# Six expert numbers packed into a word: 13 register loads ahead of the first expert loop in place of one in every tile

## The chip, the cores and the metric

The kernel runs on one core of one Trainium2 chip. The metric is the device time of one execution in microseconds, the median over several runs; lower is better. The core has five engines with an instruction stream each: TensorE (PE, with PEld for its weight loads), VectorE (DVE), ScalarE (ACT), GpSimd (POOL) and SyncE (SP, which only issues transfers here). They meet through semaphores alone: an instruction can raise one when it is complete, and another engine can wait for its value.

## What is computed

A small multimodal network over 16 sequences of 126 tokens (49 image patches and 77 words), 2016 tokens of 128 values: patch embedding, attention, a mixture of 16 experts, a two-layer LSTM-like recurrence, and a second layer of 8 experts. The change is in the first mixture of experts, which the reference writes like this (cut to what matters; `xf` holds the 2016 normalized tokens, and `h` has 512 values):

```
tw = _routing_weights(xf, Wr, br, Wgate, bgate)   # 2 of 4 groups, 2 of 4 experts in each
for e in range(16):
    h = silu(xf @ W1[e]) * (xf @ W3[e])
    out = out + tw[:, e:e + 1] * (h @ W2[e])
```

Every token therefore has four pairs with an expert, 8064 pairs in all.

## The kernel before, in words

**Routing.** The kernel sorts the 8064 pairs by expert into NT = 78 tiles of 128 rows, in such a way that a tile belongs to one expert. DVE works out in `route` how many tiles each expert gets; line 1128 leaves, for each tile on a partition of its own, the tile's expert times 2*W0 = 3072, which is where the expert's weights begin in the array `w0s`. PE turns that column into a row in PSUM (line 910, `EXPERT`). DVE and POOL then build one-hot matrices for 64 combinations of pick and token tile (lines 1141 to 1149 and 855 to 858), PE multiplies them into a table in PSUM (line 917), and from it DVE works out which rows of `x_scratch` each tile gathers (`src_row`, lines 1162 and 1163) and to which rows of `y_scratch` its result goes (`dst_row`, line 1171). Right behind the one-hot loop, at line 1152, DVE casts the row of expert offsets to integers (`expert_at`).

**The expert loop.** It is written out, not a hardware loop: 78 tiles, with every engine's instructions in an order fixed by hand. For tile i, PE waits for the transposed rows, computes the gate product (lines 937 to 939 into bank 0 or 1, raising `gate_ps`) and the up product (the same lines into bank 2 or 3, raising `up_ps`), each of three matmuls of 512 columns; then it transposes the hidden values of tile i - 1 (line 947) and multiplies those of tile i - 2 by the down weights (lines 957 and 958, raising `y_ps`). It also transposes the gathered rows of tile i + 2 (line 926, `xT_ps`), before the gate product. The matmuls read the weights at an address in a register. So PE's sequencer, the part of the engine that takes the instructions in order and hands them on, loads one offset from `expert_at` in each tile, after the up product (`expert_of`, line 930, called at line 983), and computes addresses from it with small register operations.

ACT copies the transposed rows (line 1016), applies silu (line 1033) and copies the high half of the transposed hidden values (line 1022). DVE multiplies gate and up (line 1220), forms the low half (line 1202), and adds the two halves of the down result into one of four buffers (`keep`, line 1209). PE's down product of tile i waits for `keep` of tile i - 1 (line 953), since both use one PSUM bank. POOL alternates between two indirect transfers: it fetches the rows of a tile five ahead (`fetch`, line 863) and gives the result of a finished tile (`give`, line 868). Two kinds of side work ride in the loop: in 4 early tiles ACT and DVE split weights of late experts (lines 427 and 437), and in 7 later tiles, nine apart, they split the weights of the recurrence (lines 1045 and 1231).

Behind the loop SP reads the results back, ACT and DVE mix them (lines 1051 and 1244), and the recurrence follows.

Of the kernel before, what the change touches and what calls it, by code (L numbers as in the profile page):

```python
# [18 lines left out]
I32 = mybir.dt.int32  # L19
# [53 lines left out]
YR = 4  # L73
DOWN_LAG = 2
# [16 lines left out]
def build(nc, taps_in, patches_in, txt_in, cols_in, const_in, dense_in, qkvw_in, outw_in, heads_in, w0_in,  # L91
# [5 lines left out]
    with ExitStack() as ctx:  # L97
# [123 lines left out]
        expert_at = view(NT, 1).bitcast(I32)  # L221
# [663 lines left out]
        def ffn_pe(pe):  # L885
# [25 lines left out]

            for c in range(COMBOS):
                pe.wait_ge(sg("off_hot"), c + 1)
# [15 lines left out]
            def expert_of(i):  # L929
                return nc.values_load(expert_at[0:1, i:i + 1], engines=(mybir.EngineType.PE,), min_val=0,  # L930
                                      max_val=(E0 - 1) * 2 * W0,
                                      skip_runtime_bounds_check_because="expert_f is the minimum with the last expert")
# [28 lines left out]
            pe.wait_ge(sg("route_dve"), AFTER["expert_at"])  # L961
# [36 lines left out]
        def ffn_act(act):  # L998
# [3 lines left out]
            for j in range(NBLK):  # L1002
# [6 lines left out]
                           ).then_inc(sg("route_exp"), 1)  # L1009
            act.activation(warm[:, :], warm[:, :], ACT.Silu)  # L1010
# [43 lines left out]
        def route(dve):  # L1054
# [73 lines left out]
            dve.tensor_scalar(expert_f[:, 1:2], expert_f[:, 0:1], float(E0 - 1), float(2 * W0), ALU.min, ALU.mult  # L1128
# [12 lines left out]
            for c in range(COMBOS):  # L1141
                if c >= COMBOS // 2:
                    t = c % TILES
                    dve.tensor_scalar(tile_hot[:, c, :], count16[0:SEQ, 0:NT], place[:, 1, c:c + 1],
                                      number(N_TOK + t, 1, SEQ), ALU.is_equal, ALU.mult)
                dve.tensor_scalar(off_hot[:, c, :], count16[0:SEQ, :], place[:, 2, c:c + 1], None, ALU.is_equal
                                  ).then_inc(sg("off_hot"), 1)
                if c % 4 == 0 and c < 4 * NBLK:
                    rows_low(c // 4)

            dve.wait_ge(sg("route_pe"), AFTER["expert_ps"])
            dve.tensor_copy(expert_at, EXPERT[0:1, 0:NT]).then_inc(sg("route_dve"), 1)
# [746 lines left out]
```

## Time and profile before

| what | value |
| --- | --- |
| median of 3 runs | 1110.24 us (1110.03 to 1111.13) |
| the profiled execution's own time | 1110.15 us |
| its span, first to last instruction | 1108.2 us |
| PE busy | 896.5 us, 81% of the span |
| DVE busy | 784.1 us, 71% |
| ACT busy | 556.8 us, 50% |
| POOL busy | 331.9 us, 30% |
| mean granted TensorE clock | 0.923 |

The span is what the trace shows, and 1.95 us of the execution lie around it. All times in the rows further down are microseconds from the start of the span unless marked ns. "PEldq" is the sequencer of PE; its instructions (register loads, register operations, waits) are not counted as busy. A row of a group gives the busy time, the mean of one instruction in ns, and the idle time of the engine just before, with what ended it. "<-remote" means that the idle time ended with a semaphore's update that no instruction ending near that moment explains. The clock is a share of full speed: 1.00 is 2.4 GHz and 0.50 is 1.2 GHz, and a figure between them is a stretch with some of each.

### The profile page before, as it was taken

To read this page: it belongs to the slowest core of one execution; us is meant where nothing else is said; L and a number is where in the kernel's file an instruction comes from. 1 tells how busy PE (TensorE), PEld (TensorE's weight loads), DVE (VectorE), ACT (ScalarE), POOL (GpSimd) and SP (SyncE) were. 2 spreads that over 40 slices of the span, in tenths; PEclk is the share of its full clock that TensorE was granted. 3 is DMA by queue.
4 is the path that set the end of the run, shared out by engine and by line. 5 is a ranking of instruction groups with operands and counts; after the bars stand their busy time and mean duration, and the time that the engine had idled before them with its cause. 6 is when DMAs were issued, how large, how long until landed. Compare 5 with 4: busy or idle time off the path is not lost.

```text
span 1108.2 us, 43614 instructions
## 1 busy us (share of the span) xinstructions
PE 896.5 (81%) x17230; PEld 721.4 (65%) x17230; DVE 784.1 (71%) x2835; ACT 556.8 (50%) x1629; POOL 331.9 (30%) x481
## 2 busy tenths in 40 slices
PE   3667768267787788773599999999999999989997
PEld 1346545135555555551489999999999988847786
DVE  3458984986655555556678888887788888755877
ACT  0446667125455444532354455555544455545886
POOL 0326656555565565540001111111111111020321
PEclk9769997569999998995699999999999999998999
DMA  8700005201222221216000000000000000002232
GB/s 237 271 1 2 1 30 171 62 25 38 65 66 63 65 65 44 59 34 160 19 4 0 0 0 0 0 0 0 0 0 0 0 0 0 1 2 87 94 140 75
DMA packets 26707, 52.07 MB, mean 47 GB/s; under 512 B 4528, under 2 KB 17816, under 8 KB 26648
## 3 DMA queue, kind: packets, MB, share of 16 engines
q1 hardware_dynamic: 21656, 41.04, 11.3%
q0 software_dynamic: 4992, 10.23, 3.5%
q8 instruction: 38, 0.62, 0.2%
q14 instruction: 21, 0.17, 0.0%
HBM read 44.02 MB, written 7.24 MB: 46 GB/s over the span
## 4 chain that ended last, share of the span: by engine, by line
PE 38%; DVE 10%; issue 7%; ACT 0%; DMA 0%; POOL 0%; DVEq 0%; ACTq 0%
PE quad L1330 19%; PE bank L1330 8%; DVE post L1480 3%; DVE post L1518 2%; PE quad L318 1%; PE bank L318 1%; PE quad L320 1%; PE quad L319 1%; DVE post L1524 1%; PE bank L319 1%; PE bank L320 1%; DVE post L1519 1%; PE quad L1340 1%; PE quad L1628 1%; PE bank L1360 0%
## 5 line engine op out<-in xcount | busy, mean ns | idle before, releaser
L1330 PE MATMUL quad<-post,area 128*128 128x32 f16 (+1 forms) x7520 | 230.2, 182 | 24.7 <-DVE post L1524 18.1
L1330 PEld LDWEIGHTS quad<-post,area 128*128 128x128 f16 x7520 | 213.1, 96 | 41.6 <-DVE post L1524 41.3
L1330 PE MATMUL bank<-post,area 128*128 128x32 f16 (+1 forms) x6260 | 193.2, 180 | 6.7 <-DVE post L1524 4.4
L1330 PEld LDWEIGHTS bank<-post,area 128*128 128x128 f16 x6260 | 176.9, 96 | 12.3 <-DVE post L1524 5.0
L1417 ACT ACTIVATE post<-post 128x96 f32<-128x96 f32 x252 | 71.3, 283 | 171.1 <-DVE post L1480 171.1
L1313 POOL COPY post<-post 128x32 f32 (+1 forms) x126 | 30.8, 245 | 381.8 <-DVE post L1524 381.8
L868 POOL DMA_INDIRECT y_scratch<-area x78 | 76.9, 985 | 88.7 <-DVE area L1209 78.6
L1508 DVE SCALAR_TENSOR_TENSOR post<-post 128x32 f32<-128x32 f32 x252 | 48.4, 192 | 75.6 <-ACT post L1427 75.6
L957 PE MATMUL quad<-w0s,area 128*128 x312 | 61.6, 277 | 49.2 <-DVE area L1209 49.2
L1480 DVE TENSOR_REDUCE post<-bank 128x96 f32<-128x192 f32 x252 | 80.7, 320 | 6.4 <-PE bank L1330 4.8
L1220 DVE SCALAR_TENSOR_TENSOR area<-bank,area 128x512 f32<-128x512 f32 x78 | 53.9, 691 | 43.8 <-ACT area L1033 21.3
L863 POOL DMA_INDIRECT area<-x_scratch,area x78 | 76.1, 975 | 28.1 <-issue 17.4
L1480 DVE TENSOR_REDUCE post<-quad 128x96 f32<-128x192 f32 x252 | 80.7, 320 | 5.3 <-PE quad L1330 3.8
L1016 ACT ACTIVATE area<-quad 128x256 f16<-128x256 f16 x78 | 29.9, 383 | 102.6 <-PE quad L926 59.4
L1422 ACT ACTIVATE post<-post 128x32 f32<-128x32 f32 x252 | 57.7, 229 | 29.3 <-DVE post L1480 0.2
L1202 DVE TENSOR_TENSOR area<-quad,area 128x512 f16<-128x512 f32 x78 | 53.5, 686 | 26.8 <-issue 14.4
L1427 ACT ACTIVATE post<-post 128x32 f32<-128x32 f32 x252 | 57.8, 229 | 28.1 <-DVE post L1494 0.2
L957 PEld LDWEIGHTS quad<-w0s,area 128*128 128x128 f16 x312 | 30.8, 99 | 62.1 <-issue 58.5
L1022 ACT ACTIVATE area<-quad 128x512 f16<-128x512 f32 x78 | 46.8, 600 | 41.4 <-PE quad L947 34.8
L1736 DVE TENSOR_TENSOR hidL<-area,hidH 128x504 fp32r<-128x504 f32 x64 | 49.8, 778 | 21.4 <-ACT hidH L1693 19.8
L937 PE MATMUL bank<-w0s,area 128*128 x156 | 60.7, 389 | 0.0
L938 PE MATMUL bank<-w0s,area 128*128 x156 | 60.5, 388 | 0.0
(255 smaller groups left out, 1940.4 us busy)
## 6 DMA issues: line engine op xcount, KB each, us to landing
w0s<-in_w SPq DMA_DIRECT2D x12, 768.0 KB, 12.3
area<-mask_scratch SPq DMA_DIRECT2D x7, 1008.0 KB, 4.6
area<-in_rec SPq DMA_DIRECT2D x7, 640.0 KB
post<-y_scratch SPq DMA_DIRECT2D x16, 252.0 KB
area<-in_w SPq DMA_DIRECT2D x4, 768.0 KB
post<-in_f SPq DMA_DIRECT2D x8, 256.0 KB, 4.4
area<-in_patches SPq DMA_DIRECT2D x1, 1488.4 KB
area<-in_taps SPq DMA_DIRECT2D x1, 1350.0 KB
```

The source lines that it names most:

```text
L863: pool.indirect_dma_start(xg[:, i % XG, :], None, x_dram, bass.IndirectOffsetOnAxis(src_row[:, i:i + 1].bitcast(mybir.dt.uint32), 0)).then ...
L868: pool.indirect_dma_start(y_dram, bass.IndirectOffsetOnAxis(dst_row[:, i:i + 1].bitcast(mybir.dt.uint32), 0), y_sb[:, i % YR, :], None).th ...
L937: pe.matmul(out, xh, wh, start=True, stop=False, skip_group_check=True)
L938: pe.matmul(out, xl, wh, start=False, stop=False, skip_group_check=True)
L957: pe.matmul(y_bank, hh, both, start=c == 0, stop=False, skip_group_check=True)
L1202: dve.tensor_tensor(hidT[:, i % 2, 1, :], hidT_bank[i % 2], hidT[:, i % 2, 0, :], ALU.subtract).then_inc(sg("hid_low"), 1)
L1220: dve.scalar_tensor_tensor(out=hid[:, i % 2, :], in0=bank[2 + i % 2], scalar=HID_SCALE / (H_SCALE * W_SCALE), in1=silu[:, i % 2, :], op0=A ...
L1330: mm = pe.matmul(at[0][:, at[1] + out.start:at[1] + out.stop], rec_w[:, w, s, m * P:(m + 1) * P], operand, start=False, stop=False, skip_g ...
L1417: act.activation(gates[:, l, 0:3 * SW], pre[:, l, 0:3 * SW], ACT.Tanh, scale=UNSCALE).then_inc(sg(f"gates{l}"), 1)
L1422: act.activation(gates[:, l, OUT:OUT + SW], pre[:, l, 3 * SW:4 * SW], ACT.Sigmoid, scale=UNSCALE)
L1427: act.activation(tanh_c[:, l], gates[:, l, CELL:CELL + SW], ACT.Tanh, scale=0.5).then_inc(sg(f"tanh_c{l}"), 1)
L1480: dve.tensor_reduce(pre[:, l, lo * BATCH:(lo + count) * BATCH].rearrange("p (m b) -> p m b", b=BATCH), src[:, 0:count * 64].rearrange("p ( ...
```

## The change

The offsets are no longer premultiplied: line 1128 leaves the expert's number. ACT, after PE's transpose of the expert row, multiplies every sixth entry by 16 to the power of its place (six copies of 13 elements from PSUM). DVE, after the one-hots of combination 16, adds six neighbours to one number and casts the 13 sums to integers; the cast at line 1152 goes. PE, after the table's 32nd matmul, waits for that cast and loads the 13 words into 13 registers. In the loop `expert_of(i)` is now a shift, a mask with 15 and a product with 3072 on a register, in place of a load.

```
--- before.py
+++ after.py
@@ -71,6 +71,7 @@
 XW2 = 2 * D
 XG, LOOK = 7, 5
 YR = 4
+WORD = 6
 DOWN_LAG = 2
 WHOLE = float(3 << 22)
 
@@ -218,7 +219,9 @@
         src_row = view(NT).bitcast(I32)
         dst_row = view(NT).bitcast(I32)
         expert_f = view(2, SEQ)
-        expert_at = view(NT, 1).bitcast(I32)
+        expert_row = view(NT, 1)
+        expert_sum = view(NT // WORD, 1)
+        expert_at = view(NT // WORD, 1).bitcast(I32)
         PAIR_AT = at[0]
 
 
@@ -909,7 +912,14 @@
             pe.wait_ge(sg("route_dve"), AFTER["expert_f"])
             pe.transpose(EXPERT[0:1, 0:SEQ], expert_f[:, 1:2], ident[0:SEQ, 0:SEQ]).then_inc(sg("route_pe"), 1)
 
+            words = ()
             for c in range(COMBOS):
+                if c == COMBOS // 2:
+                    pe.wait_ge(sg("route_dve"), AFTER["expert_at"])
+                    words = [nc.values_load(expert_at[0:1, w:w + 1], engines=(mybir.EngineType.PE,), min_val=0,
+                                            max_val=E0 ** WORD - 1,
+                                            skip_runtime_bounds_check_because="six experts of four bits each")
+                             for w in range(NT // WORD)]
                 pe.wait_ge(sg("off_hot"), c + 1)
                 if c < COMBOS // 2:
                     pe.wait_ge(sg("tile_hot"), c + 1)
@@ -927,9 +937,8 @@
                 mm.then_inc(sg("xT_ps"), 1)
 
             def expert_of(i):
-                return nc.values_load(expert_at[0:1, i:i + 1], engines=(mybir.EngineType.PE,), min_val=0,
-                                      max_val=(E0 - 1) * 2 * W0,
-                                      skip_runtime_bounds_check_because="expert_f is the minimum with the last expert")
+                return pe.snap((words[i // WORD] >> 4 * (i % WORD) & E0 - 1) * (2 * W0), min_val=0,
+                               max_val=(E0 - 1) * 2 * W0)
 
             def up(i, out, wh, wl, name):
 
@@ -958,7 +967,6 @@
                     mm = pe.matmul(y_bank[:, 0], hl, both[:, 0], start=False, stop=c == C0 - 1, skip_group_check=True)
                 mm.then_inc(sg("y_ps"), 1)
 
-            pe.wait_ge(sg("route_dve"), AFTER["expert_at"])
             pe.wait_ge(sg("w_low"), len(LOW_POOL))
             pe.wait_ge(sg("w_low_dve"), len(LOW_DVE) - len(LATE))
             at_of = {0: expert_of(0)}
@@ -1007,6 +1015,12 @@
             act.wait_ge(sg("route_dve"), AFTER["logit_shift"])
             act.activation(prob.rearrange("p n k -> p (n k)"), prob.rearrange("p n k -> p (n k)"), ACT.Exp
                            ).then_inc(sg("route_exp"), 1)
+            act.wait_ge(sg("route_pe"), AFTER["expert_ps"])
+            for k in range(WORD):
+                ins = act.activation(expert_row.rearrange("p (w k) -> p k w", k=WORD)[:, k],
+                                     EXPERT[0:1, 0:NT].rearrange("p (w k) -> p k w", k=WORD)[:, k], ACT.Copy,
+                                     scale=float(E0 ** k))
+            ins.then_inc(sg("route_exp"), 1)
             act.activation(warm[:, :], warm[:, :], ACT.Silu)
 
             def turned(i):
@@ -1125,7 +1139,7 @@
                                           op0=ALU.mult, op1=ALU.add))
             link(dve, dve.tensor_scalar(tiles(3), tiles(4), number(N_TOK, 1, SEQ), None, ALU.is_lt))
             link(dve, dve.tensor_reduce(expert_f[:, 0:1], tiles(3), AX, ALU.add))
-            dve.tensor_scalar(expert_f[:, 1:2], expert_f[:, 0:1], float(E0 - 1), float(2 * W0), ALU.min, ALU.mult
+            dve.tensor_scalar(expert_f[:, 1:2], expert_f[:, 0:1], float(E0 - 1), None, ALU.min
                               ).then_inc(sg("route_dve"), 1)
             for k in range(PICKS):
                 ins = dve.scalar_tensor_tensor(out=spread_pos[:, k * EW:(k + 1) * EW], in0=code,
@@ -1145,11 +1159,13 @@
                                       number(N_TOK + t, 1, SEQ), ALU.is_equal, ALU.mult)
                 dve.tensor_scalar(off_hot[:, c, :], count16[0:SEQ, :], place[:, 2, c:c + 1], None, ALU.is_equal
                                   ).then_inc(sg("off_hot"), 1)
+                if c == COMBOS // 4:
+                    dve.wait_ge(sg("route_exp"), 2)
+                    link(dve, dve.tensor_reduce(expert_sum, expert_row.rearrange("p (w k) -> p w k", k=WORD), AX, ALU.add))
+                    dve.tensor_copy(expert_at, expert_sum).then_inc(sg("route_dve"), 1)
                 if c % 4 == 0 and c < 4 * NBLK:
                     rows_low(c // 4)
 
-            dve.wait_ge(sg("route_pe"), AFTER["expert_ps"])
-            dve.tensor_copy(expert_at, EXPERT[0:1, 0:NT]).then_inc(sg("route_dve"), 1)
             dve.wait_ge(sg("route_exp"), 1)
             link(dve, dve.tensor_reduce(top_p[:, 0, :], prob, AX, ALU.add))
             link(dve, dve.reciprocal(top_p[:, 1, :], top_p[:, 0, :]))
```

## Rows read from the trace of the kernel before

**Rows 1.** The page: its first line.

```profile
span 1108.2 us, 43614 instructions
```

**Rows 2.** Busy time by stretch: bounds, length, PE, PEld, DVE, ACT, POOL; clock, DMA.

```profile
417.72:425.23 7.51, 7.51 (x63) 5.34 (x61) 4.54 (x9) 3.93 (x8) 4.99 (x6) 1.00 0.17 47
289.21:292.82 3.61, 2.67 (x23) 1.73 (x21) 3.61 (x7) 1.58 (x3) 1.95 (x3) 1.00 0.19 46
258.34:262.15 3.81, 2.68 (x24) 1.73 (x21) 3.81 (x6) 1.58 (x3) 1.97 (x3) 1.00 0.12 34
247.58:251.88 4.30, 2.71 (x24) 1.73 (x21) 4.30 (x6) 1.88 (x4) 1.99 (x3) 1.00 0.11 31
425.23:431.82 6.59, 3.58 (x24) 2.14 (x22) 3.00 (x5) 2.17 (x5) 3.22 (x5) 0.82 0.14 30
431.82:436.51 4.69, 4.69 (x22) 2.86 (x21) 1.52 (x3) 2.02 (x5) 2.78 (x3) 0.53 0.20 54
305.83:308.33 2.50, 2.50 (x23) 1.77 (x21) 1.81 (x4) 1.38 (x3) 1.89 (x3) 1.00 0.16 38
301.83:305.83 4.00, 2.67 (x23) 1.73 (x21) 1.62 (x3) 1.58 (x4) 2.01 (x3) 1.00 0.13 35
237.00:488.51 251.51, 203.44 (x1518) 135.15 (x1517) 147.93 (x253) 127.91 (x247) 144.54 (x148) 0.98 0.20 56
```

**Rows 3.** Who waited for whom, 237 to 496: us in total, times, longest.

```profile
PE quad L957 <- DVE area L1209: 49.2, 40, 2.6
...
DVE area L1209 <- remote: 33.3, 26, 1.6
```

**Rows 4.** Timeline from 301: start, duration, instruction, idle before it.

```profile
301.14 0.99 POOL L868 DMA_INDIRECT y_scratch<-area  x1 [0.30 <-issue]
...
301.66 0.22 PE L958 MATMUL quad<-w0s,area 128*128 x1
...
304.38 0.42 DVE L1209 TENSOR_REDUCE area<-quad 128x128 f32<-128x256 f32 x1 [1.61 <-remote]
304.42 0.38 ACT L1016 ACTIVATE area<-quad 128x256 f16<-128x256 f16 x1 [2.38 <-remote]
...
305.05 0.28 PE L957 MATMUL quad<-w0s,area 128*128 x1 [1.33 <-DVE area L1209]
```

**Rows 5.** PE's register load in three narrow stretches: min/median/max ns, first and last start.

```profile
L930 PEldq TENSOR_LOAD <-area x1: 298/298/298, 301.8 to 301.8; - x1
...
L930 PEldq TENSOR_LOAD <-area x1: 298/298/298, 306.2 to 306.2; - x1
...
L930 PEldq TENSOR_LOAD <-area x1: 297/297/297, 308.3 to 308.3; - x1
```

**Rows 6.** Timeline before and at the load at 306.2: POOL and ACT.

```profile
305.08 0.98 POOL L868 DMA_INDIRECT y_scratch<-area  x1 [1.69 <-DVE area L1209]
...
306.03 0.38 ACT L1016 ACTIVATE area<-quad 128x256 f16<-128x256 f16 x1 [0.25 <-PE quad L926]
```

**Rows 7.** PE's sequencer: all register loads; the register operations of one down product.

```profile
L930 PEldq TENSOR_LOAD <-area x78: 296/302/487, 227.9 to 486.1; - x78
...
L957 PEldq FUSED_REGOPS  x4: 46/46/46, 307.1 to 307.5; - x4
```

**Rows 8.** Timeline of the routing stage, 202 to 230.

```profile
202.58 0.37 PE L910 MATMUL bank<-const,area 126*1 126x126 f32 x1 [2.64 <-DVE area L1128]
...
210.49 3.39 DVE L1146 TENSOR_SCALAR area<-const,area 126x128 f16<-126x128 f16 x19
...
226.81 2.30 PE L917 MATMUL quad<-area 126*128 126x78 f16 x33 [0.40 <-DVE area L1146]
226.92 0.22 DVE L1152 CAST area<-bank 1x78 int32<-1x78 f32 x1
...
229.71 0.48 DVE L1162 TENSOR_REDUCE area<-quad 128x78 f32<-128x312 f32 x1
```

More of the change, by code:

```diff
@@ L73 @@
 YR = 4
+WORD = 6
 DOWN_LAG = 2
@@ L220, in build @@
         expert_f = view(2, SEQ)
-        expert_at = view(NT, 1).bitcast(I32)
+        expert_row = view(NT, 1)
+        expert_sum = view(NT // WORD, 1)
+        expert_at = view(NT // WORD, 1).bitcast(I32)
         PAIR_AT = at[0]
@@ L910, in ffn_pe @@
             pe.transpose(EXPERT[0:1, 0:SEQ], expert_f[:, 1:2], ident[0:SEQ, 0:SEQ]).then_inc(sg("route_pe"), 1)
+            words = ()
             for c in range(COMBOS):
+                if c == COMBOS // 2:
+                    pe.wait_ge(sg("route_dve"), AFTER["expert_at"])
+                    words = [nc.values_load(expert_at[0:1, w:w + 1], engines=(mybir.EngineType.PE,), min_val=0,
+                                            max_val=E0 ** WORD - 1,
+                                            skip_runtime_bounds_check_because="six experts of four bits each")
+                             for w in range(NT // WORD)]
                 pe.wait_ge(sg("off_hot"), c + 1)
@@ L929, in expert_of @@
             def expert_of(i):
-                return nc.values_load(expert_at[0:1, i:i + 1], engines=(mybir.EngineType.PE,), min_val=0,
-                                      max_val=(E0 - 1) * 2 * W0,
-                                      skip_runtime_bounds_check_because="expert_f is the minimum with the last expert")
+                return pe.snap((words[i // WORD] >> 4 * (i % WORD) & E0 - 1) * (2 * W0), min_val=0,
+                               max_val=(E0 - 1) * 2 * W0)
             def up(i, out, wh, wl, name):
@@ L1009, in ffn_act @@
                            ).then_inc(sg("route_exp"), 1)
+            act.wait_ge(sg("route_pe"), AFTER["expert_ps"])
+            for k in range(WORD):
+                ins = act.activation(expert_row.rearrange("p (w k) -> p k w", k=WORD)[:, k],
+                                     EXPERT[0:1, 0:NT].rearrange("p (w k) -> p k w", k=WORD)[:, k], ACT.Copy,
+                                     scale=float(E0 ** k))
+            ins.then_inc(sg("route_exp"), 1)
             act.activation(warm[:, :], warm[:, :], ACT.Silu)
@@ L1127, in route @@
             link(dve, dve.tensor_reduce(expert_f[:, 0:1], tiles(3), AX, ALU.add))
-            dve.tensor_scalar(expert_f[:, 1:2], expert_f[:, 0:1], float(E0 - 1), float(2 * W0), ALU.min, ALU.mult
+            dve.tensor_scalar(expert_f[:, 1:2], expert_f[:, 0:1], float(E0 - 1), None, ALU.min
                               ).then_inc(sg("route_dve"), 1)
```

7 lines of the change are left out of this document (4 added, 3 removed).

## The prediction

> **What bounds the kernel now.** I read four views: busy time by stretch for the pace of the expert loop, the list of waits for what breaks it, the timeline of one slow tile for the mechanism, and the sequencer's records for the register load. Durations are of the profiled execution, 1110.15 us with a span of 1108.2 [rows 1], 0.09 under the median.
>
> From the first gate matmul of tile 0 to that of tile 77, 77 tiles pass in 251.5 us, 3.27 each [rows 2]. A quick tile takes 2.50 us and PE is busy through all of it; so are three in a row with all of POOL's transfers going (7.51) [rows 2]. So 2.50 is PE's floor, 77 of them are 192.5, and 59.0 us lie above it. Taking the tiles one by one by the start of their first gate matmul, that excess divides as follows. 26 tiles take about 4.00 instead of 2.50, as the one at 301.83 does: 39.0. Seven carry a split of the recurrence's weights and take about 3.61, DVE busy throughout: 7.8. Four carry a split of late experts' weights, three of about 3.81 and one of 4.30: 5.7. Two in a row take 6.59 and 4.69, the clock going to 1.2 GHz for the second: 6.3 [rows 2]. The sum is 58.8.
>
> **The 26 tiles.** PE idles there before the down product and waits for DVE's `keep` [rows 3]. But `keep` needed only the previous down product, whose last matmul ran at 301.66 for 0.22 us; `keep` started at 304.38, and ACT's copy of the transposed rows, due at 302.0, at 304.42. Both waits end "remote" [rows 4]; DVE has 26 such before `keep`, 33.3 us in all [rows 3]. PE had done the work, then, and its semaphore updates arrived some 2.4 us late, several at once. In the rest of the kernel no wait is listed as remote.
>
> What sets these tiles apart is where the register load falls. At 301.8 it falls inside POOL's issue of a result, 301.14 to 302.13 [rows 4, 5]. At 306.2 it comes just after such an issue (305.08 to 306.06) has ended, and that tile runs at 2.50 [rows 2, 5, 6]. I laid all 78 loads beside POOL's instructions: in each of the 26 slow tiles the load overlaps a result issue, and in none of the tiles of 2.50, but for one at 422.7 just ahead of the two long ones. And the phase returns by itself: after a slow tile the load comes 0.37 after the tile's start (306.2 against 305.83), one quick tile later at its start (308.3 against 308.33) [rows 2, 5], which is inside the issue again. That is why slow and quick tiles mostly alternate. I take it that a load that meets a result issue holds back PE's updates.
>
> **The change, part by part.**
>
> *The loads in the loop go.* With the cause, the 26 holds go: 39.0. The two long tiles at 425 have late updates from PE too, the first from a load that begins just before an issue; I count them in, 6.3, less surely. The splits stay, 13.5. Gain 45.3. Next in line behind PE's 2.50 is POOL: two transfers of 0.98 with 0.30 before each [rows 4, 6] make 2.56 to 2.60 a tile. It looks ahead five tiles, and the eleven splits give it 13.5 us in which to catch up 77 x 0.08 = 6, so I charge nothing; without that cover 6 us come back.
>
> *Three register operations per tile are added.* Four stand within 0.4 us [rows 7], 0.13 apart, so three cost 0.39 of the sequencer's time, against 0.30 for a load and 0.06 to the next instruction. That is even, and the sequencer gains 0.37 on PE in a quick tile, as shown above, which covers it: nothing. If the operations weren't fused or were repeated for the down product, six would be 0.78, 0.42 more than the load, which uses that cover up and costs 0.05 a tile, 4 us in all.
>
> *Thirteen loads move ahead of the table's second half.* Its last 33 matmuls run together from 226.81 for 2.30 us, since POOL's and DVE's one-hots are done by then [rows 8]. PE's sequencer takes things in order, so the loads come after matmul 32 and push the other 32. Each takes 0.302 at the median [rows 7], 0.36 with the step behind it: 13 x 0.36 = 4.7. The table is then ready at 233.8 instead of 229.1. DVE began to read it at 229.71, 0.6 after it was ready [rows 8]; that slack stays, so 4.1 us reach DVE, POOL's first fetch and tile 0. Bounds: if loads overlap, no faster than register operations, 13 x 0.13 - 0.6 = 1.1; if each costs what the dearest did (0.487) and a step, 13 x 0.55 - 0.6 = 6.6. I take the median, since all but one lie near it. POOL issues no transfer there, so nothing should be held. The Trainium skill ("DMA: Bandwidth & Descriptors", latency and other measured facts) gives a load a floor of about 600 ns; the trace has half of that, and the trace decides. By that figure the estimate for the step would be 13 x 0.66 - 0.6 = 8 us and the forecast 4 us later.
>
> *ACT's six copies* start behind PE's transpose, done at 202.95 [rows 8]. At the 0.38 of a far larger copy [rows 4] they take 2.3 and end by 205.3. ACT has nothing urgent until the rows arrive. DVE asks for them after combination 16, past 210.49 [rows 8], so it doesn't wait; nothing is queued behind that wait in vain. DVE's sum and cast cost about 0.22 each, as the old cast did [rows 8], with links 0.6, less the 0.22 that goes: 0.4 later at the table. Its last one-hots then come 0.4 late too, at about 227.2, while PE is busy with the loads to 231.5: nothing. If the loads cost next to nothing, that 0.4 shows.
>
> *Sum:* -45.3 + 4.1 = -41.2; 1110.15 - 41.2 = 1069. Behind the loop nothing changes but the start.
>
> **Rivals.**
>
> *The holds come from POOL's issue alone.* A result issue of POOL would hold PE's updates whether a load is there or not, and the load's place only follows from the hold. Then the loop stays at 251.5, and the 4.1 us ahead of it are a loss: 1114. It decides if one quick tile in which an issue covers the down product's end is held without a load. Against it: in the quick tile of 305.83, PE's transpose ends just inside the issue of 305.08 to 306.06, and ACT goes on at 306.03 without delay [rows 6]. For it: both movers sit in one fixed order, so the phase isn't free in this trace. Beside it: the Trainium skill ("TensorE: Matmul & The Clock Gate", the per-tile semaphore tail) says that increments on completion go one after another, at 26.3 ns each, with no word of a load. Rows 4 show 2.4 us, and by that rule no load could be blamed, so that the time would be this rival's. 10%.
>
> *Half of it goes.* Holds become rarer or shorter but something late takes their place: fetches landing late, DVE's 1.8 busy of 2.50 meeting POOL's pace. A tile of 2.8 on average, 216 + 13.5 for the loop: 22 less, 18 net: 1092. For it: only short runs of quick tiles are seen. Against: in them PE never waits. 13%.
>
> *The sequencer becomes the bound.* If the mask and product were made anew at each use, eight uses x 0.39 = 3.1 us per tile minus the 0.36 and the cover of 0.37 give 2.4 more: 1069 + 185. The text of the change takes one register value per tile, which speaks against. 2%. That the words are reloaded in the loop after all, for want of registers, would leave about 1112. 2%.
>
> **How the numbers follow.** The forecast has 73%. Its own range is 1060 to 1080: below, the loads nearly free (-3) and the splits absorbed in part (-6); above, POOL's pace (+6), dear loads (+2.5) or six operations (+4), not all together. The stated range reaches to the second rival, 1060 to 1093, and leaves out the first and the dear ones. A measurement here tells about 0.2%, 2.2 us. Faster 87%, slower 11%, within it 2%.
>
> **What would show it.** Right: 13 loads at about 227 to 231, none later; the stretch of the loop at about 206 us; no wait ended remote; PE's idle before the down product near 11 us instead of 49.2 [rows 3]; DVE's L1162 near 233.9. Wrong: remote waits still there; quick tiles over 2.50 with PE waiting on sequencer ("issue"); a first gate matmul much later than 241.1.

## The result and the profile after

The changed kernel takes 1116.78 us (median of 6 runs, 1115.6 to 1121.57) where the kernel before takes 1110.55 beside it (6 runs, 1110.03 to 1112.88): a ratio of 1.0058, 95% interval 1.0038 to 1.0079 (a ratio, here and in the table below, isn't exactly that of the two medians). It is slower by some 6 us, where 41 us of gain were forecast. The profiled execution takes 1115.6 us.

The page of the changed kernel: its first line, and one of the costliest groups (busy time, mean ns of one | idle time before, and what ended most of it). L966 is the down product that was L957, L1225 `keep`; further down, L1030 is ACT's copy of the transposed rows, L866 and L871 are the fetch and the result that were L863 and L868.

```profile
span 1113.5 us, 43699 instructions
...
L966 PE MATMUL quad<-w0s,area 128*128 x312 | 61.1, 276 | 41.2 <-DVE area L1225 41.2
```

Busy time by stretch in the changed kernel, with the columns of [rows 2]: the loop from the first gate matmul of tile 0 to that of tile 77, then a quick tile, a slow one, one with a split of the recurrence's weights, and the two long ones.

```profile
246.09:494.78 248.69, 207.69 (x1519) 134.16 (x1517) 147.86 (x252) 127.56 (x247) 144.35 (x148) 0.98 0.21 56
251.37:253.87 2.50, 2.50 (x24) 1.78 (x21) 1.25 (x3) 1.65 (x4) 0.53 (x1) 1.00 0.16 51
303.92:307.85 3.93, 2.84 (x23) 1.68 (x21) 1.85 (x4) 1.99 (x5) 2.06 (x3) 1.00 0.13 34
297.77:301.41 3.64, 2.85 (x22) 1.71 (x21) 3.64 (x8) 1.58 (x3) 1.98 (x3) 1.00 0.24 50
432.52:439.53 7.01, 3.58 (x23) 2.12 (x21) 2.91 (x5) 1.85 (x4) 3.08 (x4) 0.89 0.14 28
439.53:442.94 3.41, 3.41 (x22) 2.03 (x21) 1.12 (x2) 1.55 (x4) 2.79 (x3) 0.73 0.21 61
```

The loop of 251.51 us [rows 2] is now 248.69: not 206. Who waited for whom in it, changed kernel:

```profile
ACT area L1030 <- remote: 41.3, 26, 2.3
PE quad L966 <- DVE area L1225: 41.2, 40, 3.3
DVE area L1225 <- remote: 33.0, 26, 1.6
```

The 26 remote waits of [rows 3] are still 26. One of them in the timeline of the changed kernel (start, duration, instruction, idle before it):

```profile
303.05 0.99 POOL L871 DMA_INDIRECT y_scratch<-area  x1 [0.30 <-issue]
...
303.75 0.22 PE L967 MATMUL quad<-w0s,area 128*128 x1
...
304.34 0.97 POOL L866 DMA_INDIRECT area<-x_scratch,area  x1 [0.30 <-issue]
...
306.17 0.42 DVE L1225 TENSOR_REDUCE area<-quad 128x128 f32<-128x256 f32 x1 [0.86 <-remote]
306.21 0.38 ACT L1030 ACTIVATE area<-quad 128x256 f16<-128x256 f16 x1 [1.63 <-remote]
...
306.84 0.28 PE L966 MATMUL quad<-w0s,area 128*128 x1 [1.02 <-DVE area L1225]
306.87 0.98 POOL L871 DMA_INDIRECT y_scratch<-area  x1 [1.56 <-DVE area L1225]
```

It is the picture of [rows 4] with no register load anywhere near. The down product's last matmul is over at 303.97; DVE hears of it at 306.17, 2.2 us later and 0.86 after the end of POOL's fetch issue (304.34 and 0.97). In [rows 4] it was 2.5 us. I call such a tile held. The loop is 2.8 us shorter because held tiles and the two long ones came out a little shorter in this execution. That isn't the change's doing. Over three profiles of each kernel the loop took 251.51, 247.57 and 247.24 us before (before_again and before_3, below) and 248.69, 249.42 and 248.73 after (after_again and after_3): the loads went from it, and it became no shorter.

Where the change put its loads, changed kernel: the sequencer's loads (min/median/max ns, first and last start), then PE and DVE.

```profile
L919 PEldq TENSOR_LOAD <-area x13: 295/302/479, 231.4 to 235.9; - x13
```

```profile
231.35 0.23 PE L927 MATMUL quad<-area 126*128 126x78 f16 x1 [0.39 <-DVE area L1160]
...
236.25 2.24 PE L927 MATMUL quad<-area 126*128 126x78 f16 x32 [4.67 <-issue]
...
238.59 0.48 DVE L1178 TENSOR_REDUCE area<-quad 128x78 f32<-128x312 f32 x1 [4.53 <-PE quad L927]
```

This part is as forecast: thirteen loads in 4.9 us, the table's second half behind them, and DVE idle for 4.53 us before it reads the table. Against [rows 8] that read comes 8.88 us later. Only 4.35 of these are the loads' and 0.4 the words' on DVE: the expert row's transpose, ahead of all that, already stands 4.14 later (206.72 against 202.58 [rows 8]):

```profile
206.72 0.37 PE L913 MATMUL bank<-const,area 126*1 126x126 f32 x1 [2.64 <-DVE area L1142]
```

That part is not the change's: in before_again and before_3, which are the kernel before, the same transpose starts at 206.59 and 206.67. By 190 us 3.5 of it are there, before anything that the change touches. The granted clock differs in that stage: 0.86 of full speed on average from 60 to 190 us before, 0.84 after.

```profile
60.00:190.00 130.00, 95.08 (x905) 70.10 (x906) 96.33 (x119) 87.29 (x168) 73.25 (x53) 0.86 0.13 44
```

```profile
60.00:190.00 130.00, 94.59 (x888) 69.51 (x889) 96.37 (x119) 84.06 (x166) 68.93 (x52) 0.84 0.12 42
```

(The first is the kernel before, the second the changed one.) That the clock is the cause is argued from these means, not shown. In any case this pair of profiles doesn't give the change's price; a cleaner one follows.

### The profile page after: what moved, and what is told of

Same layout as the page of the kernel before. It is cut to its first block, busy times and chain, and to the rows that moved or that the text cites. A ratio compares the mean times of both kernels' runs of the same rounds, so it can differ in the third digit from the quotient of the medians.

```text
span 1113.5 us, 43699 instructions
## 1 busy us (share of the span) xinstructions
PE 906.3 (81%) x17230; PEld 724.5 (65%) x17230; DVE 784.9 (70%) x2836; ACT 557.3 (50%) x1635; POOL 332.6 (30%) x481
## 4 chain that ended last, share of the span: by engine, by line
PE 37%; DVE 10%; issue 7%; ACT 1%; DMA 0%; POOL 0%; DVEq 0%; ACTq 0%
PE quad L1346 19%; PE bank L1346 8%; DVE post L1496 3%; DVE post L1534 2%; PE quad L321 1%; PE bank L321 1%; PE quad L323 1%; PE quad L322 1%; DVE post L1540 1%; PE bank L322 1%; DVE post L1535 1%; PE bank L323 1%; PE quad L1356 1%; PE quad L1644 1%; ACT post L1443 0%
## 5 line engine op out<-in xcount | busy, mean ns | idle before, releaser
L871 POOL DMA_INDIRECT y_scratch<-area x78 | 76.9, 985 | 86.1 <-DVE area L1225 76.0
L966 PE MATMUL quad<-w0s,area 128*128 x312 | 61.1, 276 | 41.2 <-DVE area L1225 41.2
L866 POOL DMA_INDIRECT area<-x_scratch,area x78 | 76.1, 975 | 32.5 <-issue 17.4
L1030 ACT ACTIVATE area<-quad 128x256 f16<-128x256 f16 x78 | 29.9, 383 | 102.4 <-PE quad L936 58.6
L966 PEld LDWEIGHTS quad<-w0s,area 128*128 128x128 f16 x312 | 30.6, 98 | 54.2 <-issue 50.6
L947 PE MATMUL bank<-w0s,area 128*128 x156 | 60.2, 386 | 0.0
```

The costliest lines, as they stand in the source:

```text
L866: pool.indirect_dma_start(xg[:, i % XG, :], None, x_dram, bass.IndirectOffsetOnAxis(src_row[:, i:i + 1].bitcast(mybir.dt.uint32), 0)).then ...
L871: pool.indirect_dma_start(y_dram, bass.IndirectOffsetOnAxis(dst_row[:, i:i + 1].bitcast(mybir.dt.uint32), 0), y_sb[:, i % YR, :], None).th ...
L947: pe.matmul(out, xl, wh, start=False, stop=False, skip_group_check=True)
L966: pe.matmul(y_bank, hh, both, start=c == 0, stop=False, skip_group_check=True)
```

## The experiments

The runs behind the first pair were made in six groups. The kernel before took about 1110 us in four of them, as at the start, and about 1070 in two, A and D; one chip appeared in a group of either sort, A and F. Each run is set against the kernel before in its own group. None of the eight profiles of groups A and D shows a held tile. They tell the change's own price, but nothing of what holds an update; for that only groups B, C, E and F count. Several runs of those have one time or two; within a group the times of the kernel before lie at most 11 us apart, so the 40 us between its two levels are clear even so.

| run | what it is | group | us (runs) | before beside it | ratio |
| --- | --- | --- | --- | --- | --- |
| spread | changed, loads one by one | A | 1074.82 (7) | 1070.10 | 1.0043 [1.0006, 1.0079] |
| static | before, experts fixed | A | 1070.56 (10) | 1070.10 | 1.0006 [0.9983, 1.0029] |
| sp_give | before, SP gives | A | 1068.91 (10) | 1070.10 | 1.001 [0.9984, 1.0036] |
| sp_fetch | before, SP fetches | A | 1070.9 (10) | 1070.10 | 1.0014 [0.9989, 1.0039] |
| before_again | before | B | 1108.08 (1) | 1111.10 | |
| after_again | changed | B | 1119.77 (6) | 1111.10 | 1.008 [1.0065, 1.0094] |
| sp_give_2 | as sp_give | C | 1068.98 (1) | 1111.49 | |
| sp_fetch_2 | as sp_fetch | C | 1069.89 (1) | 1111.49 | |
| static_2 | as static | C | 1119.64 (1) | 1111.49 | |
| spread_2 | as spread | C | 1113.36 (12) | 1111.49 | 1.0027 [1.0011, 1.0042] |
| pairs | before, two fetches, two results | D | 1070.54 (8) | 1070.68 | 0.9989 [0.9973, 1.0005] |
| half_fetch | before, SP fetches odd tiles | D | 1070.25 (8) | 1070.68 | 1.0004 [0.9977, 1.0031] |
| sp_give_3 | as sp_give | D | 1070.24 (10) | 1070.68 | 0.9992 [0.9976, 1.0007] |
| sp_give_after | changed, SP gives | D | 1078.54 (8) | 1070.68 | 1.0069 [1.0046, 1.0092] |
| pairs_2 | as pairs | E | 1118.09 (3) | 1109.74 | 1.0062 [1.0019, 1.0105] |
| half_fetch_2 | as half_fetch | E | 1081.96 (2) | 1109.74 | 0.9751 [0.9716, 0.9786] |
| after_3 | changed | E | 1119.1 (7) | 1109.74 | 1.0079 [1.0054, 1.0103] |
| before_3 | before | F | 1114.58 (1) | 1111.44 | |

### Is it the register loads? The kernel with no load and no register operation

`static` fixes the experts when the kernel is built (five tiles each), so it computes with weights that the routing doesn't ask for:

```
 def expert_of(i):
-    return nc.values_load(expert_at[0:1, i:i + 1], ...)
+    return i // 5 % E0 * 2 * W0
```

and takes plain slices of `w0s` in place of `bass.ds`.

> The kernel before with the tiles' experts fixed when the program is built: no register load and no register operation in the expert loop. The experts are wrong ones, so the first mixture's result is not the reference's; all other work is done. Theory A, the updates of PE are held by POOL's issue of transfers and PE's sequencer has no part in it: the slow tiles of about 4.0 us stay, 20 or more with remote waits, and the time stays within 4 us of 1110.5. Theory B, register loads or register operations of PE's sequencer hold them: no remote waits, tiles of 2.50, loop 206 us, time near 1065. By the changed kernel's trace A leads.

In group A it took 1070.56 us. Against the 1110 of the start that looks like the second of the two guesses come true, but the kernel before took 1070.10 beside it: nothing there was held, so it had nothing to show. It ran again, once, in group C:

> As static (experts fixed at build, no register load or operation in the loop, so the mixture's result is not the reference's), again, for a chip on which the kernel before takes 1110. If loads or register operations have any part in the held updates, 1070; if none, 20 or more slow tiles and 1105 to 1112. Where the kernel before takes 1070: 1070 again.

1119.64 us, above the range expected. The remote waits in its loop:

```profile
ACT area L1020 <- remote: 31.2, 14, 3.4
ACT area L1014 <- remote: 13.5, 14, 3.0
DVE area L1218 <- remote: 3.9, 1, 3.9
```

and its loop, in the columns of [rows 2]:

```profile
242.39:497.32 254.93, 209.22 (x1519) 140.22 (x1517) 148.00 (x253) 127.36 (x247) 144.53 (x148) 0.94 0.20 55
```

There are no loads in this kernel, and its loop is 3.4 us longer than the 251.51 of [rows 2]. The held tiles are fewer and longer, nine of them of 4.3 us. Here they mostly hit the update of the transposed hidden values (L1020 waits for it). A load is not needed for a hold; the changed kernel, with none in its loop and 26 held tiles, says the same.

### Is it POOL's transfers? One direction taken from POOL

`sp_give` lets SyncE give the results, to consecutive rows, and POOL only fetch; `sp_fetch` lets SyncE fetch, from consecutive rows, and POOL only give. The rows written or read are then not those that the routing asks for. The recurrence's weight loads, which SyncE issues as well, are put between them. Of `sp_give`, with the two last lines POOL's:

```
+def sp_give(i):
+    sp.wait_ge(sg("y_sb"), i + 1)
+    sp.dma_start(y_dram[i * P:(i + 1) * P, :], y_sb[:, i % YR, :]).then_inc(sg(f"y_out{i % YR}"), 16)
...
+for i in range(LOOK, NT):
+    fetch(i)
```

> The kernel before with the 78 results given by SyncE's queue, each to 128 consecutive rows of the scratch tensor instead of its own rows, so that the mixture's result is not the reference's; POOL only fetches. Theory A (POOL's issues, back to back, hold PE's updates): POOL has 1.27 of 2.50 us to do, is never back to back, the remote waits go, tiles take 2.50 and the time falls by 40 to 46 us, to 1065 to 1070. If the transfers' traffic and not their issue by POOL holds the updates, the slow tiles stay and the time is within 5 us of 1110.5.

> The kernel before with the 78 fetches made by SyncE's queue, each of 128 consecutive rows of the scratch tensor instead of the tile's own, so that the mixture's result is not the reference's; POOL only gives results. Theory A: as with the results on SyncE, no back-to-back issues, remote waits gone, time 1065 to 1070. If the result issue alone holds an update that falls inside it, whatever stands before and behind it, the slow tiles stay, since POOL's issue still begins 0.3 us after keep and covers part of the next product: 1105 or more.

In group A both are level with the kernel before: with nothing held, POOL's two transfers per tile cost nothing. In group C each ran once:

> As sp_give (results given by SyncE to consecutive rows, so the mixture's result is not the reference's), again, for a chip on which the kernel before takes 1110. There it tells the two theories of the held updates apart. Theory A (POOL's issues, a result and a fetch back to back): no remote waits, near 1067. Theory B (nothing of POOL's; the traffic or PE itself): 20 or more slow tiles, 1105 to 1112. Where the kernel before takes 1070 it tells nothing new and should repeat 1069.

> As sp_fetch (fetches by SyncE from consecutive rows, so the mixture's result is not the reference's), again, for a chip on which the kernel before takes 1110. Theory A: POOL is never back to back, no remote waits, near 1070. If the result issue alone holds PE's updates that fall into it, 1100 or more. Where the kernel before takes 1070: 1071 again.

1068.98 and 1069.89 where the kernel before took 1111.49: the 42 us are gone, with all loads still in the loop. The loop of sp_give_2, 211.59 us:

```profile
236.67:448.26 211.59, 195.79 (x1518) 135.16 (x1517) 147.35 (x253) 130.77 (x247) 69.74 (x74) 0.99 0.25 66
```

The loop of sp_fetch_2 has no remote wait. That of sp_give_2 has a few among its first tiles, where none was expected, and they matter:

```profile
242.73 0.38 PE L950 MATMUL bank<-w0s,area 128*128 x1
...
244.14 0.94 POOL L879 DMA_INDIRECT area<-x_scratch,area  x1 [0.30 <-issue]
...
245.53 0.94 POOL L879 DMA_INDIRECT area<-x_scratch,area  x1 [0.45 <-remote]
...
247.44 0.60 ACT L1044 ACTIVATE area<-bank 128x512 f32<-128x512 f32 x1 [1.31 <-remote]
```

The gate product of tile 2 (L950) is over at 243.11, and ACT's silu of it starts 4.3 us later, after 1.31 us of idling. POOL gives no results in this run: here it stands at the end of eleven fetches in a row with 0.30 between them (231.15 to 245.09). From 248 on each fetch waits for PE and stands alone, and nothing is held. So fetches alone can hold an update, when they come without a rest. In sp_fetch_2 all 78 results stand alone; whether results in a row would hold one, no run shows. What both runs took from POOL is its unbroken rows. In the profile of the kernel before, POOL issues mostly in rows of four with 0.30 between, and 26 of these 27 rows end in a hold. That isn't proof by itself, since a hold stops POOL too and so ends its row; and in groups A and D rows of up to 36 hold nothing. The two runs also changed scattered rows into consecutive ones for the direction that SyncE took over; that this plays no part is not shown.

### How much of it, and in what order?

`half_fetch` leaves three transfers in two tiles to POOL: SyncE fetches the odd tiles from consecutive rows (a ring of six tiles in place of seven). `pairs` leaves the four and changes their order:

```
-for i in range(NT):
-    if i + LOOK < NT:
-        fetch(i + LOOK)
-    if i >= 3:
-        give(i - 3)
+for i in range(0, NT, 2):
+    for j in (i + LOOK, i + LOOK + 1):
+        if j < NT:
+            fetch(j)
+    for j in (i - 3, i - 2):
+        if j >= 0:
+            give(j)
```

> The kernel before, with POOL's transfers issued two fetches, then two results, where they alternate before: the same number of issues, 2.57 us of POOL a tile. If the held updates come from a fetch that is issued directly behind a result, there is such a pair in every second tile only, and of the 26 to 28 long tiles (1.5 us each, 40 us) half go: about 1090 us where the kernel before takes 1111. If the sum of issues on POOL is what counts, nothing changes: 1111 +- 3. Where the kernel before has no held updates (1070 us), 1070 +- 3 by both.

> The kernel before, with the fetches of odd tiles issued by SyncE from consecutive rows, and those of even tiles and all results by POOL as before (a ring of six tiles in place of seven, so that a slot belongs to one queue; half of the rows fetched are not the ones that the routing asks for). POOL then issues three transfers in two tiles, 3.9 us in 5.0. If what counts is that POOL has no rest in the quick tiles, the held updates go: 1070 +- 3. If it is enough that POOL issues results and fetches in one loop, about half of the long tiles stay: 1085 to 1095. Where the kernel before has no held updates, 1070 +- 3.

Both met group D, in which nothing is held, and told nothing of this question; but the profile of `pairs` told something else. Of its 77 loads in the loop, 32 start inside POOL's issue of a result, which is more than the 26 of the profile before, and no wait of its loop ends remote. One of them, in a tile of 2.50: POOL's issue, the load in a narrow stretch around it, and the tile.

```profile
298.02 1.00 POOL L868 DMA_INDIRECT y_scratch<-area  x1 [0.30 <-issue]
```

```profile
L932 PEldq TENSOR_LOAD <-area x1: 308/308/308, 298.2 to 298.2; - x1
```

```profile
298.10:300.60 2.50, 2.50 (x23) 1.78 (x21) 1.71 (x3) 1.57 (x4) 1.90 (x2) 1.00 0.17 52
242.21:450.35 208.14, 195.75 (x1519) 135.37 (x1518) 147.18 (x252) 130.78 (x247) 148.31 (x148) 0.99 0.25 67
```

So in a group without holds a load inside an issue does nothing. Its loop of 208.14 us, with loads, is close to the 206 that I had forecast for a loop without them.

Both ran again in group E, where updates were held:

> As for the run named pairs: two fetches, then two results. With held updates in the kernel before (1111 us): about 1090 if a fetch directly behind a result is what brings them, 1111 +- 3 if the sum of issues on POOL is. Without them: 1070 +- 3 by both, and nothing is told.

> As for the run named half_fetch: the fetches of odd tiles are issued by SyncE. With held updates in the kernel before (1111 us): 1070 +- 3 if POOL's lack of rest is what counts, 1085 to 1095 if results and fetches in one loop are enough. Without them: 1070 +- 3.

`half_fetch_2` took 1081.96 us, 28 less than the kernel before. Its remote waits in the loop, and the loop:

```profile
ACT area L1041 <- remote: 4.8, 3, 1.6
```

```profile
237.51:455.55 218.04, 196.60 (x1518) 134.42 (x1517) 147.59 (x255) 127.75 (x247) 107.11 (x110) 0.99 0.22 63
```

Three remote waits are left of some 26, but the loop is still about 10 us longer than one without holds (207.97 in half_fetch). Shorter holds are at least part of that rest, in waits that the profile still puts down to PE. One of them:

```profile
305.99 0.60 PE L966 MATMUL quad<-const,area 128*128 128x128 f32 x4
...
307.48 0.60 ACT L1041 ACTIVATE area<-quad 128x512 f16<-128x512 f32 x1 [1.34 <-PE quad L966]
```

The transposes are over at 306.59, and ACT's copy starts 0.89 later, at the end of a result issue of POOL (306.49 and 0.98). In sp_give_3 the same step takes 0.04. In half_fetch_2 twelve of ACT's 78 copies of this kind, the three remote ones among them, and eight of its row copies start more than 0.6 us late after an idle wait; in half_fetch none does. (Of these twenty, 19 have a load inside a result issue beside them, but in the one shown the load starts at 307.25, when the update has been due for 0.66.) The time lies between the two guesses (1070, and 1085 to 1095): POOL's want of rest counts for most of it.

`pairs_2` took 1118.09, above both guesses, with 22 and 3 such waits before its two ACT copies: no gain from the order, rather a loss. The idea that a fetch directly behind a result is the trigger, which gave 1090, falls. And the load and the hold have come apart, in a group with holds. Ahead of the 22 remote waits of the row copy in pairs_2 the last load starts inside a result issue once, inside a fetch issue 17 times and between issues 4 times.

### What does the change cost by itself?

`after_again` and `after_3` are the changed kernel once more, `before_again` and `before_3` the kernel before.

> The kernel before, unchanged, for a profile: the last four runs had it at 1070 us beside them, not 1110. Theory A, the held updates belong to a chip or a time and not to the program: its time is near 1070 with no remote waits and tiles of 2.50, or near 1110 with 20 or more slow tiles, nothing between. Theory B, the time of 1070 beside those runs had some other reason than the slow tiles: a loop of 251 us and yet a time near 1070.

> The changed kernel, unchanged, beside the kernel before on the same chip. If no updates are held, the change can only cost: 4.5 us for the 13 loads ahead of matmul 32, 0.4 for DVE's sum and cast, and about 2 in the loop for register operations in the tiles that carry a split (3.87 us in the run with the loads spread, 3.68 in one with loads in the loop), together 6 to 7 over the kernel before. If the change frees the loop of anything that the kernel before still has, it is faster than that kernel by more than 2 us.

> The changed kernel. With held updates in the kernel before (1111 us): 1117 to 1120, ratio 1.006 to 1.008. Without them (1070 us): the change only adds, so 1077 +- 2, ratio 1.0065 +- 0.002; by the forecast's account, in which the loads are what the loop is to be rid of, level with or below the kernel before.

> The kernel before. If it takes about 1070 us: no wait ends remote, first to last gate matmul 207 to 208 us, seven tiles of 3.68 and four of 4.0, all others 2.50, though its 78 register loads still stand in the loop and some of them meet a result issue of POOL. If it takes about 1110 us, 26 to 28 held tiles as in the profile of before, and nothing new is told.

Ratios of 1.008 and 1.0079: somewhat more than the first 1.0058, and that is 8.7 and 9.4 us. (The 6 to 7 expected of after_again were for a loop without holds.) `before_3` met held tiles again (28 remote waits before ACT's copy), so the kernel before has no profile without them, and its loop in that case is known only through its neighbours.

The clean pair is sp_give_3 and sp_give_after in group D: the kernel before and the changed kernel, with the same edit that lets SyncE give the results, and nothing held in either.

> The kernel before, with results given by SyncE to consecutive rows and POOL fetching alone (the rows written are not the ones that the routing asks for). No held updates: 1069 +- 2 on whichever chip.

> The changed kernel with the same edit as the run before it: results given by SyncE to consecutive rows, POOL fetching alone. If the change's loads in the loop were part of what held updates cost, this would be level with the run before it. By the theory that the change only adds (13 loads in a row ahead of table matmul 32 4.35 us, two word operations on DVE 0.4, register operations in the tiles that split 2), it is 6 to 7 us slower than the run before it: 1075.5 +- 2, ratio between them 1.006.

1070.24 and 1078.54: 8.3 us between them and 1078.54 itself above the 1075.5 +- 2 expected, and 8.0 between the spans (1068.8 and 1076.8). Of each a loop and one tile with a split; first sp_give_3:

```profile
241.18:448.66 207.48, 194.35 (x1519) 134.97 (x1518) 147.41 (x254) 130.94 (x247) 69.95 (x74) 0.99 0.26 68
311.53:315.22 3.69, 2.68 (x24) 1.73 (x22) 3.69 (x7) 1.60 (x4) 0.94 (x1) 1.00 0.16 44
```

The same of sp_give_after:

```profile
247.02:456.66 209.64, 196.96 (x1519) 135.04 (x1517) 147.49 (x253) 130.86 (x247) 69.71 (x74) 0.99 0.26 67
318.31:322.17 3.86, 2.84 (x23) 1.70 (x21) 3.86 (x8) 1.61 (x4) 0.94 (x1) 1.00 0.17 46
```

The 8.0 us divide like this. 0.7 was there ahead of the table already, so isn't the change's. At table matmul 32 it is 0.85: the words cost 0.16. DVE's read of the table is 5.61 later: the loads cost 4.76. The first gate matmul is 5.84 later (0.23 more), and the loop takes 209.64 in place of 207.48, 2.16 more. Behind it nothing is added. The 2.16 lie in the eleven tiles with splits: seven of 3.70 on average that become 3.89, four of 4.02 that become 4.23. `static` in group A, with neither loads nor register operations, has 3.57 for the same kind of tile:

```profile
311.08:314.65 3.57, 2.66 (x24) 1.74 (x22) 3.57 (x7) 1.60 (x4) 2.63 (x3) 1.00 0.42 75
```

DVE is busy through all of such a tile in each of the three kernels, and its work isn't longer: from the start of the splits to `keep` it takes 1.47 in all three. What differs is PE behind `keep`. The end of the tile in sp_give_3, where L937 are the transposes of the next rows and L948 begins the gate product, and what PE's sequencer does for L948:

```profile
315.10 0.28 PE L937 MATMUL quad<-const,area 128*128 128x128 f16 x2
315.22 0.38 PE L948 MATMUL bank<-w0s,area 128*128 x1
```

```profile
L948 PEldq FUSED_REGOPS  x1: 42/42/42, 315.1 to 315.1; - x1
```

The same in sp_give_after, where the two are L947 and L957:

```profile
321.88 0.28 PE L947 MATMUL quad<-const,area 128*128 128x128 f16 x2
322.17 0.39 PE L957 MATMUL bank<-w0s,area 128*128 x1
```

```profile
L957 PEldq ALU_OP  x2: 36/38/41, 321.9 to 322.0; - x2
L957 PEldq FUSED_REGOPS  x1: 46/46/46, 322.1 to 322.1; - x1
```

In a tile with a split PE's sequencer stands at the wait for `keep`, so its lead is gone when the wait ends. Two register operations more than in sp_give_3 then stand just before the gate product: 0.29 us from the transposes to it in place of 0.12. That is the 0.17 by which this tile is longer. The 0.12 between 3.57 and 3.69 isn't the load either, which was over before that wait: nearly all of it is one address operation between the wait and the down product (0.21 from wait to matmul, 0.11 in static). In a quick tile, where the sequencer is ahead, neither costs anything: 2.50 in all three kernels.

### Can the loads be hidden?

`spread` issues the thirteen loads one by one between table matmuls, in the gaps in which PE waits for one-hots anyway:

```
-if c == COMBOS // 2:
-    pe.wait_ge(sg("route_dve"), AFTER["expert_at"])
-    words = [nc.values_load(expert_at[0:1, w:w + 1], ...) for w in range(NT // WORD)]
+w = c - COMBOS // 4 - 2
+if w == 0:
+    pe.wait_ge(sg("route_dve"), AFTER["expert_at"])
+if 0 <= w < NT // WORD:
+    words += [nc.values_load(expert_at[0:1, w:w + 1], ...)]
```

> The changed kernel with its 13 word loads taken one per combination, from the 18th of the table's matmuls on, where PE waits 0.4 to 0.6 us for every one-hot; nothing is left out. If the loads' place ahead of matmul 32 costs the changed kernel 4.5 us (13 x 0.36 less slack), this run's table is ready right behind the last one-hots, the last 32 matmuls follow the 32nd without a gap, and the time is 4 to 5 us under the changed kernel's, 1112 us. If the loads cost PE's sequencer time wherever they stand, the gap only moves and the time stays at 1116 to 1117. The loop keeps its 26 slow tiles under either.

> As spread (the changed kernel with its 13 loads one per combination), again, for a chip on which the kernel before takes 1110 and the changed one 1117 to 1120. The place of the loads is worth 4.5 us there too: 1112 to 1115, that is 1 to 4 us over the kernel before.

The loads in spread_2, and the table's last matmuls:

```profile
L921 PEldq TENSOR_LOAD <-area x13: 294/300/484, 222.9 to 230.3; - x13
```

```profile
231.56 2.30 PE L928 MATMUL quad<-area 126*128 126x78 f16 x33 [0.40 <-DVE area L1161]
...
238.91 0.37 PE L937 MATMUL quad<-const,area 128*128 128x128 f16 x2 [5.04 <-DMA area<-x_scratch,area]
```

The thirteen are spread over 7.4 us, and the last 33 matmuls run together as in [rows 8], with no gap. Matmul 32 starts 24.63 us after the expert row's transpose, exactly as in the changed kernel, whose loads come later: the spread loads delay nothing. With held tiles the loss is 1.9 us, where the changed kernel's is 8.7 and 9.4 in the neighbouring groups; without them it is 4.7 (group A, with an interval from 0.6 to 8.5), where the clean pair's is 8.3. That the thirteen loads in a row are the larger part of the change's price is shown; what remains is a small loss, about what the splits cost. No version with packed words beat the kernel before.

## Why the prediction was wrong

**The step that failed** is "I take it that a load that meets a result issue holds back PE's updates", and with it "With the cause, the 26 holds go: 39.0". The loads went and 26 remote waits stayed. In place of the load, POOL issuing its transfers without a rest is what the runs tie to the held updates: with either direction moved to SyncE the loop lost 40 us, all loads still in it.

The evidence was a coincidence in all of 26 tiles and in almost none of the others. I called the return of the phase the reason why slow and quick tiles alternate; it was the reason why the coincidence was complete. PE and POOL both run through a fixed order, and each hold sets them to the same places again: once a hold comes at a certain place in POOL's transfers, the load of that tile always stands at the same place beside them. The load's position followed from the hold. The changed kernel and static_2 show holds with no load, and pairs_2 shows them with loads that stand elsewhere. (That `pairs` has the same meeting 32 times with no hold says less, since nothing was held in its group.)

**The rival that came true** is "the holds come from POOL's issue alone", given 10%. Its price, 1114, is 2.8 under what was measured. It named a result issue; sp_fetch_2 has 78 of them, each by itself, and no hold, and in sp_give_2 it was fetches in a row. So the rival had the engine right and not the trigger. It had even named its own condition for deciding, and the sentence "the phase isn't free in this trace" was the reason to weigh it far more.

By the Trainium skill ("TensorE: Matmul & The Clock Gate", the per-tile semaphore tail) each increment on completion adds 26.3 ns, with nothing in it for a load. In the conclusion that a load is not to blame the runs agree with it; the 2.2 us of a held update stand in no such tail.

**The two long tiles**, 6.3 us, "counted in, less surely": 7.01 and 3.41 against 6.59 and 4.69 [rows 2]. Of the 6.3, 0.9 went in this execution. Part of them ran at 1.2 GHz again (mean clocks of 0.89 and 0.73, against 0.82 and 0.53).

**The splits stay**: they did, but not at their price. "Nothing" for the three register operations is wrong in those eleven tiles by 2.2 us, and right in all others. The cover that I named, the sequencer's lead in a quick tile, was real there; I didn't ask for it in a tile in which the sequencer waits for `keep`, and there it is gone.

**The thirteen loads**: 4.1 forecast at DVE's read, 4.35 in the first pair of profiles and 4.76 in the clean one. Steps of 0.36 were right. The median, not the bounds, was the value to take; and by the Trainium skill's floor of about 600 ns ("DMA: Bandwidth & Descriptors", latency and other measured facts) the estimate would have been 8. The trace decides: 302 ns at the median, and 0.36 from one to the next.

**The words on DVE**: 0.4 forecast, hidden; 0.4 and 0.16 measured, and not hidden, since what they delay is table matmul 32, behind which the loads stand.

**No charge for POOL's pace**: right. With nothing held, POOL's two transfers a tile cost nothing against one (`sp_give`, ratio 1.001).

The sum with the holds left in is 4.76 for the loads, 0.16 for the words and 2.16 in the loop: 7.1, with the 0.23 at the first tile 7.3. Against that stand 8.0 between the spans of the clean pair, of which 0.7 isn't the change's, and 6.2, 8.7 and 9.4 us beside the kernel before with holds. The forecast's floor, 1069, is about what the kernel before takes by itself when nothing is held (1070.10 and 1070.68). It has nothing to do with the change.

## What to carry to other kernels

When a trace blames one event by always standing beside another, ask whether the two can move apart at all in that trace. In a fixed order of work that settles into a cycle, everything coincides with everything; ask for the one tile where the suspect is there without the effect, and without such a tile give the rival its half. The cheapest check is a kernel without the suspect and with all else in place, as `static` is, set against the unchanged kernel in the same group of runs: without that neighbour its first time would have confirmed the wrong cause.

Moving small waits out of a loop to a place ahead of it is a gain only if that place has slack. Thirteen loads in series behind one matmul stood on the path in full; one by one in gaps of 0.40 us they were free. And a sequencer's lead covers its small operations only while it has one: look for the tile in which it has just waited.

## What the runs showed of the hardware

**Held updates.** When POOL issues indirect transfers without a rest, PE's semaphore updates can arrive late, mostly by 2 to 3 us. In the profiles of the kernel before and of the changed one they come about 0.9 us after the end of a fetch issue of POOL (0.86 in the tile shown above); in static_2 some come earlier than that. With both directions on POOL the kernel takes 1111 us, with either one moved to SyncE 1069 to 1070, with three of four transfers left on POOL 1082. Results aren't needed for it: eleven fetches in a row were enough in sp_give_2. And it isn't always there: in two of six groups of runs the kernel before takes 1070 and no profile shows it, with rows of up to 36 issues, and in one case on a chip that showed it in another group. What switches it on I couldn't find, and whether the late part is PE's sending or the receivers' hearing isn't settled by these traces. It is worth 40 us here, far more than any edit of this study.

**A register load by PE** takes 0.30 us, in a row 0.36 each, and doesn't overlap the next; the first of the thirteen took 0.48.

**POOL's one-hots have two paces.** In after_3, table matmul 32 comes 3 us later than in the other runs of the changed kernel, since POOL takes 0.75 us for a one-hot and not 0.62. The same 21 in after_3 and in sp_give_3:

```profile
218.27 15.84 POOL L859 TENSOR_SCALAR area<-numbers,area 126x78 f16<-126x78 f32 x21
```

```profile
218.56 13.04 POOL L872 TENSOR_SCALAR area<-numbers,area 126x78 f16<-126x78 f32 x21
```

DVE's 64 one-hots beside it get done sooner in that case, in 20.4 us and not 21.5 (after_3 and after). Of the twenty profiles of this study two have the slow pace, after_3 and half_fetch_2, so it isn't the change's doing; but it is part of why a single profile of the changed kernel can be off by 3 us.
